# Splitting the last out projection tile of an attention step nine and three instead of six and six

## The reference

```python
q = rope((x @ Wq.T)); k = rope(x @ Wk.T); v = x @ Wv.T            # per head
scores = einsum('bhnid,bhnjd->bhnij', qc, kc)                     # in a chunk of 128
y_intra = einsum('bhnij,bhnjd->bhnid', scores * decay, xc)
state   = state * chunk_decay + k_dec.T @ xc                      # chunk to chunk
y_inter = (qc * exp(G)) @ state
y = y_intra + y_inter
y = y / sqrt(mean(y*y, axis=-1) + eps) * gnorm_w                  # the squares are summed here
y = y * silu(x @ Wg.T)
out = y.reshape(B, L, H * D) @ Wo.T                               # the out projection
```

## Time and profile before

| | us |
|---|---|
| median of 3 runs | 2358.24 |
| the profiled execution's own time | 2350.6 |
| its span in the profile | 2348.8 |
| TensorE matmuls busy | 2134.9 (91%) |
| TensorE weight loads busy | 1687.2 (72%) |
| VectorE busy | 1836.9 (78%) |
| ScalarE busy | 1403.2 (60%) |
| GpSimd busy | 1076.4 (46%) |

### The profile page before, as it was taken

The page is one execution under the profiler, slowest core; times in us unless marked ns, Lnnn a source line. Parts: engine busy times, 40 slices in busy tenths (PEclk is TensorE's granted clock), DMA queues, the critical chain, the costliest instruction groups (busy, mean ns, idle before and its releaser), DMA issues.

```text
span 2348.8 us, 35057 instructions
## 1 busy us (share of the span) xinstructions
PE 2134.9 (91%) x9788; PEld 1687.2 (72%) x9788; DVE 1836.9 (78%) x3422; ACT 1403.2 (60%) x2716; POOL 1076.4 (46%) x840
## 2 busy tenths in 40 slices
PE   6599999999999999996999999999999999777884
PEld 6477777777777777774777777777777777555653
DVE  3488888888888888865888888888888888466665
ACT  2366666666666666653666666666666666455550
POOL 6245454545354544443454555454545455422216
PEclk9899999999999999997999999999999999898897
DMA  4312121212121212124121212121211121387777
GB/s 171 128 41 64 36 63 36 70 37 63 36 63 36 63 36 66 41 77 157 40 68 36 63 36 63 36 63 37 65 45 54 49 53 50 113 259 247 251 238 237
DMA packets 155566, 198.61 MB, mean 85 GB/s; under 512 B 13831, under 2 KB 90215, under 8 KB 155518
## 3 DMA queue, kind: packets, MB, share of 16 engines
q1 hardware_dynamic: 139742, 163.86, 23.8%
q0 software_dynamic: 7424, 21.00, 3.0%
q10 hardware_dynamic: 8352, 13.17, 1.5%
HBM read 169.65 MB, written 28.33 MB: 84 GB/s over the span
## 4 chain that ended last, share of the span: by engine, by line
issue 41%; POOL 26%; DVE 11%; PE 8%; DMA 7%; ACT 3%; SPq 2%; POOLq 1%; DVEq 0%; ACTq 0%
POOL gm L687 5%; POOL zl L425 5%; DMA gate<-in_wm 4%; POOL ql L694 3%; POOL wol L646 3%; POOL wgl L646 3%; POOL wql L646 2%; POOL vl L708 2%; DVE vwl L1557 1%; DMA gbc<-decay_exponents 1%; POOL kl L694 1%; DVE ql L1789 1%; POOL wkvl L646 1%; ACT qh L1030 1%; DVE yb L1501 1%
## 5 line engine op out<-in xcount | busy, mean ns | idle before, releaser
L425 POOL TENSOR_TENSOR zl<-yb,zh 128x512 fp32r<-128x512 f32 x130 | 172.6, 1328 | 348.5 <-ACT zh L872 348.3
L1085 PE MATMUL OU<-woh,zh 128*128 128x512 f32 x520 | 243.8, 469 | 16.3 <-POOL wol L646 11.9
L1085 PE MATMUL PJ<-xnh,wqh 128*128 128x512 f32 x544 | 225.9, 415 | 24.4 <-DVE t L1538 22.6
L1536 DVE TENSOR_TENSOR t<-PJ,cosb 128x512 f32<-128x512 f32 x160 | 110.2, 689 | 176.0 <-PE PJ L1087 132.8
L1087 PE MATMUL PJ<-xnh,wql 128*128 128x512 f32 x544 | 215.8, 397 | 0.0
L1086 PE MATMUL PJ<-xnl,wqh 128*128 128x512 f32 x544 | 215.3, 396 | 0.0
L890 ACT ACTIVATE qh<-t 128x512 fp32r<-128x512 f32 x128 | 81.0, 633 | 221.5 <-DVE t L1541 221.5
L1085 PE MATMUL PJ<-xnh,wgh 128*128 128x512 f32 x512 | 204.7, 400 | 0.0
L1087 PE MATMUL OU<-woh,zl 128*128 128x512 f32 x520 | 204.5, 393 | 0.0
L1086 PE MATMUL OU<-wol,zh 128*128 128x512 f32 x520 | 204.0, 392 | 0.0
L1087 PE MATMUL PJ<-xnh,wgl 128*128 128x512 f32 x512 | 200.4, 391 | 0.0
(11 more groups left out here) (479 smaller groups left out, 6550.9 us busy)
## 6 DMA issues: line engine op xcount, KB each, us to landing
gbc<-decay_exponents SPq DMA_DIRECT2D x128, 256.0 KB, 4.8
gate<-in_wm SPq DMA_DIRECT2D x48, 512.0 KB, 4.5
stage<-in_wq SPq DMA_DIRECT2D x72, 256.0 KB, 3.9
stage<-in_wg SPq DMA_DIRECT2D x64, 256.0 KB, 2.7
stage<-in_wo SPq DMA_DIRECT2D x64, 256.0 KB, 2.7
gbc<-in_wm SPq DMA_DIRECT2D x48, 256.0 KB, 4.1
expert_rows<-rs ACTq DMA_DIRECT2D x48, 256.0 KB, 4.1
stage<-in_wkv SPq DMA_DIRECT2D x34, 256.0 KB, 2.7
```

The lines of the kernel that those rows point to most:

```text
L425: nc.gpsimd.tensor_tensor(lo[:], yb[:, c, :], hi[:].bitcast(F32), ALU.subtract).then_inc(S["zlo"], 1)
L1085: nc.tensor.matmul(out_, a_hi, b_hi, start=first, stop=False)
L1536: v.tensor_tensor(t1[:], PJ[bank][:], cosb[:], ALU.mult)
```

## The change

The first part of the fourth tile takes three heads instead of two (nine matmuls instead of six), the second part one instead of two (three instead of six). No instruction is added or removed, and no wait is moved to another instruction.

```diff
                             if c < 2:
                                 out_proj(at, c + 1)
                             elif c == 2:
-                                out_proj(at, 3, range(HG // 2))
-
-                        out_proj(at, 3, range(HG // 2, HG))
+                                out_proj(at, 3, range(HG - 1))
+
+                        out_proj(at, 3, range(HG - 1, HG))
                         squares(3)
```

## The result

The changed kernel takes 2378.96 us (median of 4 runs, 2377.94 to 2379.65) against 2356.91 us of the kernel before (4 runs, 2355.04 to 2359.32). The ratio is 1.0093, 95% interval 1.0075 to 1.0110: 22.05 us slower, and by the interval between 17.7 and 25.9. The forecast was 2380.1 us, or +21.9.

The account below looks back on a forecast made before the run. The prediction took TensorE to bound the attention steps: 32 steps x 0.684 us = 21.9 us on the median of 2358.24 us gives 2380.1 us (+0.93%), range 2370 to 2388 us.

Parts of the forecast that it names:

- TensorE is the bound: In the attention steps TensorE, busy 853.92 of 880 us, bounds the kernel; its pauses cost time unless later taken back.
- The chain of 2.22 us: From squares(2) through ScalarE's copy and square to squares(3): 2.22 us, not shortened, so TensorE stands 0.684 us more.
- Nothing to fill at the other end: Ahead of inter(3) and intra(3), no pause shortens the longer first part; covered time 0, at most 0.07 us.
- 0.684 us per step: Three out projection matmuls of 0.228 us each; squares(3) and all behind it on TensorE start that much later, 32 times.
- Nothing hides it: In the next step VectorE, ScalarE and GpSimd start from squares(3) or the projection behind it, each 0.684 us later.
- the three pauses: Idle weight loads of 0.54, 1.11 and 0.94 us in the next step, claimed not to swallow the delay.
- The base: Forecast made from the median before, 2358.24 us, which lies 7.6 us above the profiled execution's own 2350.6 us.
- The signs: In the profile after: squares(3)'s load idle 0.94 us, near 30 us in all; squares(2) to squares(3) 2.23 us; TensorE's busy time unchanged.
- The range: Stated as 2370 to 2388 us for the whole kernel, its lower end taken down to reach the partly hidden case.
- Partly taken back: Rival: the next step's pauses absorb the delay in one kind of step, leaving 10.9 us, 2369 us; chance 5%.
- Not slower because intra(3) waits already: Rival: the moved matmuls fill a wait for wfl ahead of intra(3), so the change costs nothing, 2358 us; chance 4%.
- The clock: Rival: the new pause lowers TensorE's clock in each of 32 steps, 64 us on top, 2444 us; chance 3%.

Follow-up runs that it names:

- fill_9_3: Changed kernel plus three matmuls with an unused product, into idle bank CS ahead of squares(3): 2381.33 us, ratio 1.0114 to the kernel before.
- fill_6_6: Kernel before plus three matmuls with an unused product, into bank CS ahead of squares(3): 2373.19 us, ratio 1.0080.
- s12_0: Kernel before with the whole fourth tile (twelve matmuls) in its first part and nothing between squares(2) and squares(3): 2401.40 us, ratio 1.0198.
- short_9_3: Changed kernel with squares(3) writing bank CS and ScalarE's square of chunk 3 ahead of its copy: 2365.16 us, ratio 1.0040 to the kernel before.
- s3_9: Kernel before with the fourth tile split the other way, three matmuls in its first part and nine in its second: 2377.22 us, ratio 1.0085.
- short_6_6: Kernel before with squares(3) writing bank CS and ScalarE's square of chunk 3 ahead of its copy: 2351.58 us, ratio 0.9985.

## Why the prediction was right

- *TensorE is the bound, a pause there is time of the kernel.* Right: the same three matmuls cost nothing where TensorE stands (fill_9_3) and nearly their full length where it doesn't (fill_6_6, 0.58 us in a typical step). That the wait grew by 22.0 us and the time by 22.05 is partly luck: the interval is 4 us wide to either side, and in s12_0 the two differ by 12 us (56.9 and 45.2).
- *The chain of 2.22 us is not shortened by the move.* Right in the changed kernel (2.23 us) and with no matmul at all between (2.22 us); short_9_3 shows that it is this chain and no other, since cutting 0.50 us out of it gave back most of the time.
- *Nothing to fill at the other end.* Right: the distances into inter(3) and intra(3) are 0.23 and 0.11 us in both kernels. How near wfl was cost something only when the first part was made shorter (s3_9).
- *0.684 us per step.* A little small. 20.3 us over 31 steps is 0.65, but the one interval that has the shared expert between the halves was 0.6 us shorter; the other thirty gained 20.9 us, 0.70 each. From squares(1) to squares(2), with the first part between them, the median of the 32 steps went from 4.29 to 5.00 us, 0.71 more. In the first part of the changed kernel four matmuls in a row take 0.93 us (732.61 to 733.54), 0.233 each and not 0.228, and three of these are 0.70. That the forecast of 21.9 us met the measured 22.05 so closely is luck: the 31 steps and the last one give 21.0, and the interval of the medians spans 8 us.
- *Nothing hides it.* Right: the three pauses are the same to 0.02 us, and both kinds of step grew alike (56.53 to 57.25 us and 56.70 to 57.41). At twice the delay (s12_0) they still took nothing.
- *The base.* The profiled execution was forecast at 2372.5 us of its own time and took 2378.28. Its span is 27.7 us longer than before: 20.3 in the 31 steps, 0.7 in the last, 7.6 in the part with the experts, and 0.9 less ahead of the steps. The 7.6 us are in code that did not change, and the medians grew by 22.05 only.
- *The signs.* The 0.94 us, 30 us in all and 2.23 us came out as said. TensorE's busy time did not stay the same, it rose by 16.6 us, for the reasons given with the page; its share went from 90.9% to 90.5%, which the page rounds to 91% in both.
- *The range.* The likeliest case's own range was worked out as 2373 to 2389 us, and the stated one ends at 2388 without a reason; nothing hangs on it here.
- *The rivals.* Partly taken back: no. Not slower because intra(3) waits already: no, though the wait was 0.07 us away. The clock: 1.00 from 131 to 1000 us and from 1150 to 1900 us in all ten kernels, with idle weight loads of up to 2.03 us in each step of s12_0. In the first steps of the second half it was lower in the kernel before already (0.87 from 1050 to 1100 us and 0.86 from 1100 to 1150; 0.90 and 0.83 in the changed one). The Trainium skill, "TensorE: Matmul & The Clock Gate", section "A second HAM failure mode: psum-queue depth-cycling", warns that frequent short gaps make the clock go back and forth; in these two stretches no trace here shows it.

## What to carry to other kernels

When filler work is split between two places of a saturated engine, each part is cover for its own chain on the other engines: read for both how far the input is ahead of the instruction that needs it, before moving anything. Here these margins were 0.07 us and nothing, so a move of three matmuls (0.70 us) cost about 0.7 us per step one way and about 0.6 the other. Where both are used up, shortening the chain (another bank, the square ahead of the copy) gains what reordering the filler can't, and an engine that starts each step from the delayed instruction passes the whole delay on.

## What the runs showed of the hardware

A weight load that comes only when its matmul is due cost about 0.1 us here: the float32 matmul of squares(3) is recorded 1.12 to 1.13 us long with the load late and 1.02 us with it early, and 0.55 against 0.46 us pass until the next start. This holds in both banks (TR late in the kernel before and early in s3_9, CS late in short_9_3 and early in short_6_6). It makes no difference whether the load is late by a hair (0.26 us of idle weight loads in the kernel before) or by much: with 2.03 us of idle the record is 1.13 us as well.

The float32 matmul of squares(2) costs more than the distance to the next start shows. Behind squares(2) the next matmul starts after 0.45 us, but the one after that 0.64 us later instead of 0.23. Together that is 1.09 us for the two, so squares(2) costs about 0.86 us (1.09 less 0.23) when work follows it.
